# Graph network with two layers: 80 instead of 72 node tiles counted, 80 instead of 108 edge blocks gathered

## The chip, the cores and the metric

One core of one Trainium2 chip runs the whole program. Times are device microseconds of one execution. The kernel before takes 6933.1 us, the median of 3 runs (6923.75 to 6956.05).

## What is computed

The graph has 12500 nodes with 64 features and 400000 edges, sorted by target `dst`, each with 32 features; on the mean 32 edges end in a node. Cut to what matters:

```python
edge_index = jnp.stack([src, dst])
h = relu(layernorm(x))
x = x + L0(h, edge_index, edge_attr_32, ...)   # messages by an MLP with layer norm, summed by target, update
h = relu(layernorm(x))
x = x + L1(h, edge_index, W1, b1, W2, b2)

def L1(x, edge_index, W1, b1, W2, b2):         # the second layer
    src, dst = edge_index
    agg = segment_sum(x[src], dst, num_segments=x.shape[0])
    h = x + agg                                # (1 + 0) * x + agg
    return maximum(h @ W1 + b1, 0) @ W2 + b2
```

The change is about `agg` of the second layer.

## The kernel before

The program is a row of stages with a barrier between them: setup, the first layer's messages, the update of the nodes, the second layer's sums, and its MLP. Each stage is written as one instruction list per engine (PE, ACT, DVE, POOL, SP), and semaphores with counted values hold these together. The order of the work on each engine is written out by hand.

The second layer's sums go into `cT`, the nodes' features with the nodes along the columns. There are two ways to a sum, and both run at once.

**Counted tiles.** The last `TILES` = 72 of the 98 tiles of 128 nodes each (from tile `T0`) get their sums without a gather. For each tile a matrix of counts (source by target) is made: the keys of up to 64 edges a node lie in `keyl` and `keyh`; DVE makes one-hots of them in 8 groups of 8 (`one_hot_pairs`, L1675 and L1677), PE multiplies these in 16 chunks of 4 matmuls (`pairs`, L1619), ACT copies each chunk's counts from PSUM to `cnt` (L1568). PE then multiplies the counts of the tile before with the nodes' features, split into three bf16 parts (`product`, 100 matmuls at L1598, spread over chunks 2 to 15), ACT copies the result (`raw_sums`, L1560, at chunk 0), PE turns it and adds its parts (`turn`, L1609, at chunk 4), and DVE adds it to `cT` (`add_tile`, L1665, after group 5). Pairs write two PSUM buffers in turn, so the pairs of a chunk wait for ACT's copy of the chunk two before; the one-hots have two buffers also.

**Gathered blocks.** The nodes before tile `T0` get their sums from the first `ITER * GN` = 36 * 3 = 108 blocks of 1024 edges. ACT writes a block's indices (`index`, L792), POOL issues 8 indirect DMAs of 128 rows each (L740), DVE makes the one-hots of the targets in a window of 40 nodes (`hots`, L779), PE multiplies them in 4 fp32 products, 8 matmuls in the profile (`window_sums`, L772), and DVE adds even and odd halves to the window of `cT` (`add_block`, L812 and L816). Edges of these blocks that belong to a counted tile are marked so that no column matches.

The loop's body is two tiles, `s` = 0 and 1, with three blocks. Where the blocks' steps stand in it is in four tables: `SUMS` gives PE's chunk of each block's sum (block 0 at chunk 8 of tile 0, blocks 1 and 2 at chunks 3 and 13 of tile 1), `NEXT` ACT's chunk of the index for the next round, `HOTS` and `ADDS` DVE's group of one-hots and adds. A block's buffers are one of three (`gat`, one-hots), its sums one of two PSUM buffers.

In the update stage before, POOL gathers the tiles' keys (`node_edges`, L1253, one indirect DMA a tile, 16 tiles a chunk of the stage, so 8 in the last chunk), in between the copies that feed PE (L1262); DVE masks them (L1419, L1423), PE turns them (L1306), and ACT copies them to `keyl` and `keyh` (L1363).

Of the kernel before, what the change touches and what calls it, by code (L numbers as in the profile page):

```python
# [16 lines left out]
def build_gnn(nc, x, src, dst, src_rows, dst_rows, dst_heads, head_cols, edge_quads, W1, b1, g1, be1, W2, b2, Wu, bu, gn, bn, M1, c1, M2, c2, out):  # L17
# [8 lines left out]
    BLOCKS, BC = src.shape[1], src.shape[2]  # L26
    EB = 128 * BC
    UN = 4
# [6 lines left out]
    T = N // TP  # L35
    Q = 4
    CH = 20 if T % 20 == 0 else Q
    CHUNKS = T // CH
    BQ = CH // Q
# [3 lines left out]
    COLS = dst_rows.shape[1] - 1  # L43
    E = COLS * 128
    SLOTS = 64
    NT = -(-N // 128)
    TILES = 72
    T0 = NT - TILES
    ITER = TILES // 2
    GN = 3  # L50
    HEAD = 8
    HQ = 20
    KC = COLS // 125
# [2 lines left out]
    GPS = 64 // GP  # L56
    GW = 128
    assert EB == 8 * 128 and COLS == 125 * KC and (HEAD * KC) % HQ == 0 and COLS % CHUNKS == 0 and ITER * GN <= BLOCKS
    assert CHUNKS == BQ and GN < UN and NT <= 98 and TILES % 2 == 0 and 4 * T <= 512 and (BLOCKS - 1) * BC < COLS <= BLOCKS * BC
    assert BC % 4 == 0 and T % CH == 0 and CH % Q == 0 and F == 64 and ED == 32 and TP * Q <= 512  # L60

    ctx = ExitStack()
    with ctx:
# [180 lines left out]
        def wait(eng, semaphore, value):  # L244

            if not isinstance(value, int) or value > 0:
                eng.wait_ge(semaphore, value)  # L247
# [567 lines left out]

            return v.tensor_tensor(to, to, of[F:2 * F, WIN:2 * WIN], ALU.add)  # L816

        def before(j):

            return 1 if j == 0 else 2  # L820

        DB = 2 * UN

        def lagged(e, j, lag):
# [663 lines left out]
        k_add = sem("l1_sums_added")  # L1488
# [12 lines left out]

        CHS = 16
        FIRST_PART = 2
        SUMS = ({8: 0}, {3: 1, 13: 2})
        NEXT = ({10: 0}, {5: 1, 15: 2})
        HOTS = ({6: 1}, {4: 2, 7: 3})
        ADDS = ({1: -1, 6: 0}, {3: 1})
        TURN_AT, ADD_AT = 4, 5

        def two(body):  # L1510
# [15 lines left out]
        def first(d, n):  # L1526

            return isinstance(d, int) and d < n

        with nc.Block() as block:  # L1530
# [16 lines left out]
            @block.scalar  # L1547
            def _(a):
                def index(r, j):
                    n = r * GN + j  # L1550

                    wait(a, k_sum, n - GN + 1)
                    indices(a, n, 0, j).then_inc(k_idx, 1)

                def raw_sums(d):

                    wait(a, d_sum, d + 1)

                    wait(a, d_turn, d)
                    a.activation(raw[:, :], wide, ACT.Copy).then_inc(d_raw, 1)  # L1560

                def tile(d, s, e):
                    for ch in range(CHS):
                        wait(a, d_use, d * CHS + ch + 1)
                        if ch == 0:

                            wait(a, d_sum, d - 1)
                        a.activation(cnt[0:TP, s, ch * 8 * T:(ch + 1) * 8 * T].rearrange("p (b k) -> p b k", b=2),  # L1568
                                     built[ch % 2][0:TP, :, :], ACT.Copy).then_inc(d_copy, 1)
                        if ch == 0 and not first(d, 2):  # L1570
                            raw_sums(d - 2)
                        if ch in NEXT[s] and not (isinstance(e, int) and e == ITER - 1):
                            index(e + 1, NEXT[s][ch])
                with a.If(flagged(a) == 0):
                    for j in range(GN):
                        index(0, j)
                    tiles(a, tile)
                    raw_sums(TILES - 2)
                    raw_sums(TILES - 1)

            @block.tensor
            def _(pe):
                def sums(r, j):
                    n = r * GN + j
                    wait(pe, g_gat[j], r * (16 * BC) + L0_ROWS + 16 * BC)
                    wait(pe, k_oh, n + 1)

                    wait(pe, k_add, n + 1 - before(j))
                    window_sums(pe, j, gat[:, j, :, :], agl[j % 2]).then_inc(k_sum, 1)

                def product(d, s, lo, hi):
# [32 lines left out]
                def tile(d, s, e):  # L1624
                    for ch in range(CHS):
                        pairs(d, ch)
                        if ch == TURN_AT and not first(d, 2):
                            turn(d - 2)
                        if ch in SUMS[s]:
                            sums(e, SUMS[s][ch])  # L1630
                        if ch >= FIRST_PART and not first(d, 1):
                            parts = CHS - FIRST_PART
                            product(d - 1, 1 - s, (ch - FIRST_PART) * T // parts, (ch - FIRST_PART + 1) * T // parts)
# [7 lines left out]
            def _(v):  # L1641
                def hots(r, j):
                    n = r * GN + j

                    wait(v, k_sum, n + 1 - GN)
                    one_hot(v, j, block_of(rel_all, n)).then_inc(k_oh, 1)

                def add_block(r, j, groups):
                    n = r * GN + j

                    wait(v, k_sum, n + 1)
                    wait(v, k_add, n)
                    wait(v, d_add, groups)
                    to = window_of(v, n)
                    add_even(v, to, agl[j % 2]).then_inc(k_even, 1)
                    v.wait_ge(k_even, n + 1)
                    add_odd(v, to, agl[j % 2]).then_inc(k_add, 1)

                def add_tile(d, blocks):
                    wait(v, d_turn, d + 1)  # L1660
                    wait(v, k_add, blocks)
                    wait(v, d_add, d)
                    at = (T0 + d) * 128
                    to = cT[0:F, at:at + GW] if isinstance(d, int) else cT[0:F, bass.ds(at, GW)]
                    v.tensor_tensor(to, to, turned, ALU.add).then_inc(d_add, 1)  # L1665
# [14 lines left out]
                def tile(d, s, e):  # L1680
                    for g in range(GPS):
                        one_hot_pairs(d, g)
                        if g in ADDS[s]:
                            j = ADDS[s][g]
                            if j >= 0:

                                add_block(e, j, d - 1 if g > ADD_AT else d - 2)
                            elif not first(e, 1):
                                add_block(e - 1, GN - 1, d - 2)
                        if g == ADD_AT and not first(d, 2):  # L1690
                            add_tile(d - 2, e * GN + (0 if s == 0 else 2))
                        if g in HOTS[s]:
                            j = HOTS[s][g]
                            if j < GN:
                                hots(e, j)
                            elif not (isinstance(e, int) and e == ITER - 1):
                                hots(e + 1, 0)
                with v.If(flagged(v) == 0):
                    hots(0, 0)
                    tiles(v, tile)  # L1700
                    add_block(ITER - 1, GN - 1, TILES - 2)
                    add_tile(TILES - 2, ITER * GN)
                    add_tile(TILES - 1, ITER * GN)

# [131 lines left out]
```

## Time and profile before

| | us |
|---|---|
| Median of 3 runs | 6933.1 |
| The profiled execution | 6930.31 |
| Its span, first to last instruction | 6928.6 |
| Setup, first layer and update, to the first pairs of the second layer | 5067.9 |
| The second layer's sums, 72 tiles | 1678.1 |
| The second layer's MLP | 182.6 |
| PE / PEld / DVE / ACT / POOL busy over the span | 4087.1 / 3298.2 / 2515.7 / 1807.5 / 4280.7 |

A window's row gives its length, then for each engine the busy time and the number of instructions, the clock that was granted to PE as a share of full speed (1.00 is 2.4 GHz, 0.50 is 1.2 GHz), and the DMA traffic. In a timeline a row is an engine's instructions of one line in a row: start, length, engine, line, what was written and read, their number, and in brackets the idle time before them with what ended it. PEld is the weight load that overlaps PE. The tiles of the second layer's sums can be told apart by their pairs, L1619: 64 matmuls a tile, 4 a chunk, with no product between those of chunks 0 and 1.

### The profile page before, as it was taken

What the parts mean: (1) busy time and instruction counts of PE and PEld (TensorE: products, weight loads), DVE (VectorE), ACT (ScalarE), POOL (GpSimd) and SP (SyncE); (2) the same over time, 40 slices, a digit from 0 to 9 for tenths busy, and PEclk for the clock granted to TensorE, in tenths of its full rate; (3) what the DMA queues carried; (4) which work ended last, traced back from release to release, by engine and by line L of the source; (5) the groups of instructions that cost most, each with busy time, mean ns of one, the idle gap of its engine ahead of it and who ended that gap; (6) DMA issues with size and microseconds to landing.
All of it is one profiled execution on the core that took longest, in us unless ns stands there. A gap on an engine that the chain in (4) does not pass through costs nothing. (4 is left out here: it accounts for less than half of the span.)

```text
span 6928.6 us, 75131 instructions
## 1 busy us (share of the span) xinstructions
PE 4087.1 (59%) x24926; PEld 3298.2 (48%) x24926; DVE 2515.7 (36%) x5227; ACT 1807.5 (26%) x2517; POOL 4280.7 (62%) x4190
## 2 busy tenths in 40 slices
PE   5344544544554544555455455456658888788789
PEld 4233333433443433333334333335547777777776
DVE  5222222222222222222222222223656666566551
ACT  1011111111111111111111111111246555555551
POOL 3766666666666666666666666664456655556551
PEclk9556656666665666666566666666579999999995
DMA  2111111111111111111111111111110000000001
GB/s 84 42 34 34 34 34 34 35 33 34 34 35 33 35 34 34 35 34 35 33 34 34 33 35 35 33 34 23 40 23 18 18 17 16 17 17 17 17 17 34
DMA packets 257339, 216.92 MB, mean 31 GB/s; under 512 B 139070, under 2 KB 189563, under 8 KB 256617
## 3 DMA queue, kind: packets, MB, share of 16 engines
q0 software_dynamic: 133248, 136.74, 9.1%
q1 hardware_dynamic: 123881, 77.59, 3.9%
q8 instruction: 106, 1.74, 0.1%
q14 instruction: 104, 0.85, 0.0%
HBM read 199.53 MB, written 14.40 MB: 31 GB/s over the span
## 5 line engine op out<-in xcount | busy, mean ns | idle before, releaser
L740 POOL DMA_INDIRECT gat<-layer_rows,idx x3992 | 4050.5, 1015 | 2172.5 <-issue 1207.8
L765 PE MATMUL ps<-w2d,edge_buffers 128*128 128x128 f32 x3128 | 718.5, 348 | 868.9 <-issue 853.6
L1008 DVE TENSOR_TENSOR edge_buffers<-ps,gat 128x512 f32<-128x512 f32 x391 | 270.5, 692 | 2454.5 <-remote 1428.9
L1568 ACT ACTIVATE node_buffers<-ps 125x800 bf16<-125x800 f32 x1152 | 947.0, 838 | 703.8 <-PE ps L1619 553.5
L765 PEld LDWEIGHTS ps<-w2d,edge_buffers 128*128 128x128 f32 x3128 | 561.7, 241 | 1071.1 <-issue 1070.6
L772 PE MATMUL ps<-one_hots,edge_buffers 128*128 128x80 f32 x3128 | 604.4, 326 | 563.8 <-issue 543.2
L772 PEld LDWEIGHTS ps<-one_hots,edge_buffers 128*128 128x128 f32 x3128 | 593.4, 252 | 645.2 <-issue 615.5
L748 PE MATMUL ps<-w1e,edge_buffers 128*128 128x256 f32 x1564 | 616.0, 509 | 395.8 <-issue 263.1
L967 ACT ACTIVATE edge_buffers<-ps,gcol 128x512 f32<-128x512 f32 x391 | 302.6, 774 | 2088.1 <-remote 1730.9
L1619 PE MATMUL ps<-node_buffers 128*128 128x200 bf16 x4608 | 644.3, 265 | 333.3 <-ACT node_buffers L1568 188.3
L1598 PE MATMUL ps<-edge_buffers,node_buffers 125*128 125x192 bf16 x7200 | 811.5, 256 | 1.7 <-issue 1.2
L1598 PEld LDWEIGHTS ps<-edge_buffers,node_buffers 125*128 125x128 bf16 x7200 | 704.7, 142 | 16.5 <-issue 14.8
L1675 DVE TENSOR_TENSOR node_buffers<-iol,node_buffers 128x1024 bf16<-128x1024 bf16 x576 | 399.3, 693 | 633.4 <-PE ps L1619 454.1
L748 PEld LDWEIGHTS ps<-w1e,edge_buffers 128*128 128x128 f32 x1564 | 366.1, 255 | 521.9 <-issue 484.1
L1619 PEld LDWEIGHTS ps<-node_buffers 128*128 128x128 bf16 x4608 | 412.6, 102 | 420.0 <-issue 256.4
L755 PE MATMUL ps<-ident,node_buffers 128*128 128x128 f32 x1564 | 354.9, 329 | 402.5 <-issue 396.3
L1677 DVE TENSOR_TENSOR node_buffers<-ioh,node_buffers 128x1600 bf16<-128x1600 bf16 x576 | 567.8, 986 | 0.0
L974 ACT ACTIVATE edge_buffers<-ps 128x512 f32<-128x512 f32 x391 | 233.0, 596 | 976.7 <-remote 795.6
L755 PEld LDWEIGHTS ps<-ident,node_buffers 128*128 128x128 f32 x1564 | 241.1, 182 | 446.0 <-issue 443.3
L812 DVE TENSOR_TENSOR cT<-cT,ps 64x40 f32 x499 | 92.9, 186 | 901.8 <-remote 615.8
L953 ACT ACTIVATE node_buffers<-edge_buffers 128x2048 f32<-128x2048 f32 x98 | 187.2, 1910 | 837.1 <-DVE edge_buffers L1008 717.2
L1031 DVE TENSOR_TENSOR node_buffers<-edge_buffers,st 128x512 f32<-128x512 f32 x391 | 267.7, 685 | 3.3
(186 smaller groups left out, 2952.4 us busy)
## 6 DMA issues: line engine op xcount, KB each, us to landing
gat<-layer_rows,idx POOLq DMA_INDIRECT x3992
edge_buffers<-in_edge_quads SPq DMA_DIRECT2D x391, 128.0 KB
node_buffers<-in_x SPq DMA_DIRECT2D x5, 625.0 KB
layer_rows<-node_buffers SPq DMA_DIRECT2D x25, 125.0 KB
residual_rows<-node_buffers SPq DMA_DIRECT2D x5, 625.0 KB
layer_rows<-node_buffers SPq DMA_DIRECT2D x5, 625.0 KB
node_buffers<-residual_rows POOLq DMA_DIRECT2D x25, 125.0 KB, 4.4
out<-node_buffers SPq DMA_DIRECT2D x25, 125.0 KB
```

The source lines that it names most:

```text
L740: pool.indirect_dma_start(out=gat[:, j, c, :], out_offset=None, in_=table[:, :], in_offset=bass.IndirectOffsetOnAxis(ap=idx[:, half, j, c: ...
L748: mm = pe.matmul(o[:, k * 4 * F:(k + 1) * 4 * F], ea[:, j, k, :], w1e[:, :], start=True, stop=True)
L755: mm = pe.transpose(o[:, k * 128:(k + 1) * 128], zn[:, j, 2 * k:2 * k + 2, :].rearrange("p c f -> p (c f)"), ident[:, :])
L765: mm = pe.matmul(o[:, k * 128:(k + 1) * 128], hT[:, j, k * 128:(k + 1) * 128], w2d[:, :], start=False, stop=(k == PAIRS - 1), skip_group_c ...
L772: mm = pe.matmul(to[:, 0:2 * WIN], rows_of[:, 2 * k:2 * k + 2, :].rearrange("p c f -> p (c f)"), oh[:, j, 2 * k:2 * k + 2, :].rearrange("p ...
L967: a.activation(hT[:, s, :], tp[(j - HID) % 2][:, 0:PAIRS * 128], ACT.Silu, bias=gcol[:, 1:2], scale=gcol[:, 0:1]).then_inc(g_h, 1)
L1008: v.tensor_tensor(zb[:, j // UN % 2, s, :, :], zp[j % 2][:, 0:BC * F].rearrange("p (c f) -> p c f", c=BC), gat[:, s, :, :], ALU.add).then_ ...
L1568: a.activation(cnt[0:TP, s, ch * 8 * T:(ch + 1) * 8 * T].rearrange("p (b k) -> p b k", b=2), built[ch % 2][0:TP, :, :], ACT.Copy).then_inc ...
L1598: mm = pe.matmul(wide, cnt[0:TP, s, t:t + (GW - 1) * T + 1:T], hparts[:, t, :, :].rearrange("p k f -> p (k f)"), start=(t == 0), stop=(t = ...
L1619: mm = pe.matmul(built[ch % 2][:, i // 2, (i % 2) * 2 * T:(i % 2 + 1) * 2 * T], ohl[:, ch // 2 % 2, k // 2, :, k % 2], ohk[:, ch // 2 % 2, ...
L1675: v.tensor_tensor(ohl[:, g % 2, :, :, :], iol[:, :, :].unsqueeze(1).broadcast_to([128, GP // 2, 128, 2]), spread(keyl, d, g, 128), ALU.is_ ...
L1677: v.tensor_tensor(ohk[:, g % 2, :, :, :], ioh[:, :, :].unsqueeze(1).broadcast_to([128, GP // 2, 2 * T, 2]), spread(keyh, d, g, 2 * T), ALU ...
```

## The change

80 tiles are counted, from tile 18 on, and 80 blocks gathered, two a loop body: block `s` in tile `s`, through two buffers. In each tile PE takes the sum at chunk 1 instead of 8, 3 or 13, ACT the next round's index at chunk 3, DVE the adds after group 2 and the next one-hots after group 4. The add of a tile's sums waits for the block of the same tile. The separate add of the last block behind the loop is gone. The keys take 8 tiles more.

```diff
-    TILES = 72
+    TILES = 80
     T0 = NT - TILES
     ITER = TILES // 2
-    GN = 3
+    GN = 2
...
-        def before(j):
-
-            return 1 if j == 0 else 2
...
-        SUMS = ({8: 0}, {3: 1, 13: 2})
-        NEXT = ({10: 0}, {5: 1, 15: 2})
-        HOTS = ({6: 1}, {4: 2, 7: 3})
-        ADDS = ({1: -1, 6: 0}, {3: 1})
+        SUM_AT, NEXT_AT, BLOCK_AT, HOT_AT = 1, 3, 2, 4
         TURN_AT, ADD_AT = 4, 5
...
-                        if ch in NEXT[s] and not (isinstance(e, int) and e == ITER - 1):
-                            index(e + 1, NEXT[s][ch])
+                        if ch == NEXT_AT and not (isinstance(e, int) and e == ITER - 1):
+                            index(e + 1, s)
...
-                    wait(pe, k_add, n + 1 - before(j))
+                    wait(pe, k_add, n + 1 - GN)
...
-                        if ch in SUMS[s]:
-                            sums(e, SUMS[s][ch])
+                        if ch == SUM_AT:
+                            sums(e, s)
...
-                def add_block(r, j, groups):
+                def add_block(r, j, d):
                     n = r * GN + j
 
                     wait(v, k_sum, n + 1)
                     wait(v, k_add, n)
-                    wait(v, d_add, groups)
+                    wait(v, d_add, d - 2)
...
-                        if g in ADDS[s]:
-                            j = ADDS[s][g]
-                            if j >= 0:
-
-                                add_block(e, j, d - 1 if g > ADD_AT else d - 2)
-                            elif not first(e, 1):
-                                add_block(e - 1, GN - 1, d - 2)
+                        if g == BLOCK_AT:
+                            add_block(e, s, d)
                         if g == ADD_AT and not first(d, 2):
-                            add_tile(d - 2, e * GN + (0 if s == 0 else 2))
-                        if g in HOTS[s]:
-                            j = HOTS[s][g]
-                            if j < GN:
-                                hots(e, j)
+                            add_tile(d - 2, e * GN + s + 1)
+                        if g == HOT_AT:
+                            if s == 0:
+                                hots(e, 1)
                             elif not (isinstance(e, int) and e == ITER - 1):
                                 hots(e + 1, 0)
                 with v.If(flagged(v) == 0):
                     hots(0, 0)
                     tiles(v, tile)
-                    add_block(ITER - 1, GN - 1, TILES - 2)
                     add_tile(TILES - 2, ITER * GN)
                     add_tile(TILES - 1, ITER * GN)
```

## Rows read from the trace of the kernel before

**Rows 1.** Windows of stages: us, busy (x instructions) per engine, PEclk, DMA

```profile
5067.90:5133.80 65.90, 36.64 (x252) 28.59 (x253) 27.48 (x40) 25.67 (x34) 43.86 (x40) 0.63 0.09 21
5133.80:6715.10 1581.30, 1283.75 (x12558) 1177.93 (x12557) 972.15 (x1485) 923.50 (x1277) 952.22 (x824) 0.92 0.08 17
6715.10:6746.00 30.90, 27.57 (x301) 26.08 (x299) 12.50 (x22) 14.19 (x20) 0.00 (x0) 0.99 0.01 3
6746.00:6928.60 182.60, 178.82 (x500) 114.84 (x500) 19.32 (x50) 33.90 (x50) 33.09 (x25) 0.50 0.19 36
```

**Rows 2.** Windows of single tiles; engines PE, PEld, DVE, ACT, POOL

```profile
5530.58:5550.01 19.43, 16.73 (x181) 15.46 (x180) 14.10 (x23) 13.34 (x20) 11.81 (x11) 1.00 0.07 15
5550.01:5574.35 24.34, 18.09 (x188) 16.27 (x187) 14.04 (x22) 13.17 (x19) 14.52 (x14) 1.00 0.09 20
5574.35:5592.85 18.50, 16.56 (x182) 15.48 (x179) 14.08 (x23) 13.32 (x20) 12.20 (x10) 1.00 0.08 16
6234.07:6250.93 16.86, 16.22 (x180) 15.47 (x179) 14.07 (x23) 13.43 (x20) 12.83 (x10) 1.00 0.08 18
6368.26:6392.71 24.45, 19.76 (x180) 18.34 (x178) 13.59 (x22) 13.00 (x18) 11.25 (x10) 0.83 0.05 12
...
6715.06:6732.13 17.07, 16.58 (x182) 15.84 (x181) 11.98 (x20) 12.84 (x17) 0.00 (x0) 1.00 0.02 4
```

**Rows 3.** Waits, 6715.06 to 6732.13: waiting, released by, us, times, longest

```profile
PE ps L1619 <- ACT node_buffers L1568: 0.5, 1, 0.5
```

**Rows 4.** Waits, 5550.01 to 5574.35

```profile
ACT node_buffers L1568 <- PE ps L1619: 6.7, 6, 2.0
...
PE ps L1619 <- ACT node_buffers L1568: 5.5, 5, 2.0
```

**Rows 5.** Timeline from 5584.4, in the tile from 5574.35

```profile
5584.49 0.53 PE L1619 MATMUL ps<-node_buffers 128*128 128x200 bf16 x4
...
5586.29 0.95 POOL L740 DMA_INDIRECT gat<-layer_rows,idx  x1 [0.30 <-issue]
5586.49 0.84 ACT L1568 ACTIVATE node_buffers<-ps 125x800 bf16<-125x800 f32 x1 [2.50 <-PE ps L1619]
```

**Rows 6.** Timeline of PE in the last tile, without gathers

```profile
6716.51 0.54 PE L1619 MATMUL ps<-node_buffers 128*128 128x200 bf16 x4 [0.49 <-ACT node_buffers L1568]
...
6723.44 0.75 PE L1598 MATMUL ps<-edge_buffers,node_buffers 125*128 125x192 bf16 x7
...
6724.39 0.82 PE L1598 MATMUL ps<-edge_buffers,node_buffers 125*128 125x192 bf16 x8
```

**Rows 7.** Timeline of POOL: a run of 8 gathers, and the next one's start

```profile
5560.84 0.94 POOL L740 DMA_INDIRECT gat<-layer_rows,idx  x1 [3.33 <-ACT idx L792]
...
5570.58 0.94 POOL L740 DMA_INDIRECT gat<-layer_rows,idx  x1 [0.30 <-issue]
5575.63 0.94 POOL L740 DMA_INDIRECT gat<-layer_rows,idx  x1 [4.11 <-ACT idx L792]
```

**Rows 8.** Timeline of DVE and PE: a group of one-hots, a block's sums

```profile
5258.12 0.69 DVE L1675 TENSOR_TENSOR node_buffers<-iol,node_buffers 128x1024 bf16<-128x1024 bf16 x1 [3.51 <-PE ps L1619]
...
5258.73 0.99 DVE L1677 TENSOR_TENSOR node_buffers<-ioh,node_buffers 128x1600 bf16<-128x1600 bf16 x1
...
5259.27 1.04 PE L772 MATMUL ps<-one_hots,gat 128*128 128x80 f32 x8
...
5260.15 1.06 PE L1598 MATMUL ps<-edge_buffers,node_buffers 125*128 125x192 bf16 x6
```

**Rows 9.** Timeline of PE: the first block's sums

```profile
5080.96 1.99 PE L772 MATMUL ps<-one_hots,gat 128*128 128x80 f32 x8 [5.64 <-DMA gat<-layer_rows,idx]
```

**Rows 10.** Timeline of the update stage's last chunks: ACT, and DVE's masks

```profile
4992.42 0.38 ACT L1329 ACTIVATE node_buffers<-ps 125x256 f32<-125x256 f32 x1 [4.50 <-PE ps L1284]
...
5019.81 1.22 DVE L1419 TENSOR_TENSOR node_buffers<-iol,deg 128x1024 bf16<-128x1024 bf16 x1
...
5047.58 0.68 DVE L1419 TENSOR_TENSOR node_buffers<-iol,deg 128x512 bf16<-128x512 bf16 x1
```

More of the change, by code:

```diff
@@ L58, in build_gnn @@
     assert EB == 8 * 128 and COLS == 125 * KC and (HEAD * KC) % HQ == 0 and COLS % CHUNKS == 0 and ITER * GN <= BLOCKS
-    assert CHUNKS == BQ and GN < UN and NT <= 98 and TILES % 2 == 0 and 4 * T <= 512 and (BLOCKS - 1) * BC < COLS <= BLOCKS * BC
+    assert CHUNKS == BQ and GN == 2 and NT <= 98 and TILES % 2 == 0 and 4 * T <= 512 and (BLOCKS - 1) * BC < COLS <= BLOCKS * BC
     assert BC % 4 == 0 and T % CH == 0 and CH % Q == 0 and F == 64 and ED == 32 and TP * Q <= 512
```

## Prediction

> **What bounds the kernel now.** I read the table of stretches first [rows 1]. 1678.1 of the 6928.6 us are the second layer's aggregation, from 5067.9 to 6746.0. Its 72 tiles of 16 chunks run between two barriers, so what a tile takes more or less arrives in full at the end; the MLP behind it (182.6 us, PE busy 178.8) is one chain on PE that the edit does not touch. From the third tile to the last one's start it is 1581.3 us for 69 tiles, 22.9 us each, with 824 gather instructions, 12 a tile. No engine fills it: PE 81%, DVE 61%, ACT 58%, POOL 60%.
>
> So what takes the rest? I took windows of single tiles [rows 2]. Tiles of nearly the same work differ by half. The one from 6234.07 has one block sum, 10 gathers, and nothing late: 16.86 us. The one from 6715.06 is the last: its two sums still come, but no gather is left, and it takes 17.07 us to its last pairs, about 17.8 to where a next tile would begin. The others have 10 to 14 gathers and take 18.5 to 24.5 us. Two things are to be seen: time grows with gathers, and where the granted clock is 0.83 it grows again (24.45 against 18.50 us, both with 10 gathers).
>
> The waits [rows 3, 4] say what is late. In the tile without gathers PE waited 0.5 us for ACT's copies; in the tile from 5550.01 it waited 5.5 us for them, and ACT 6.7 us for PE. Each waits for the other, which is no full engine but a late hand-over. The timeline shows one [rows 5]: the pairs of 5584.49 end at 5585.02, yet ACT's copy of them begins at 5586.49, after 2.50 us of idle, amid a run of gathers. Without gathers [rows 6] the chunks follow each other every 0.95 us (products at 6723.44 and 6724.39). I therefore read the stage as PE's chain of chunks plus a loss that comes with gathers. That is a correlation; why the hand-over is late I can't say.
>
> **The price of a run of gathers.** A clean pair of tiles is 16.86 + 17.8 = 34.7 us. The pair 5530.58 to 5574.35 took 43.77 us at clock 1.00, and its three blocks' gathers come in runs of 8 with 3 to 4 us between them [rows 2, 7]: (43.77 - 34.7) / 3 = 3.0 us a run. The tile from 5574.35 has one late hand-over, at the end of the run that began 1.3 us into it: 18.50 - 16.86 = 1.6 us. Over the whole stretch, slow clock included, a pair takes 45.8, a loss of 11.1 us, 3.7 us a block. So a run costs 1.6 to 3.7 us, and nothing in the tile of 16.86 us.
>
> **Part by part, in a tile.** (a) 80 blocks in place of 108: one sum and one run of 8 gathers a tile instead of one and a half. A sum is 8 matmuls, 0.88 us of PE (5259.27 to 5260.15, [rows 8]). (b) The sum moves to chunk 1. PE idles there already: the pairs of chunk 2 wait for ACT's copy, 0.49 us before 6716.51 [rows 6]. So half of the sum falls into that hole, and a clean tile is 16.86 - 0.5 = 16.4 us. (c) DVE adds the block after its group 2. It starts that group when chunk 1's pairs are done and needs 0.69 + 0.99 us for it [rows 8], by which time the 0.88 us of sums are over: its wait is near 0. Queued behind it on DVE are the later groups, one needed every 1.9 us (two chunks) for 1.68 us of work; the block's two short adds and the one-hots of group 4 take that slack, at worst 0.2 us a tile, in the range. (d) The index at chunk 3 releases POOL at once (the sum it waits for was two chunks before); 8 gathers take some 11 us (5560.84 to 5571.52, [rows 7]) and are wanted nearly two tiles later, so PE waits for rows only at the start. (e) A sum's wait for the add two blocks back and the tile's add's wait for this tile's block are met a tile, or three groups, before: 0. (f) Eight tiles more, whole, with all they cost.
>
> (g) The loss. One run a tile, with some 7 us of rest after it. It will start near chunk 4, later than the run that cost 1.6 and earlier than the one in the middle of a tile, which cost most. I take 2.4, between 1.6 and 3.0. A tile is 16.4 + 2.4 = **18.8 us**.
>
> **Start, end, and the stage before.** The first two tiles took 65.9 us [rows 1]. PE stood 5.64 us there for the first gathered block, at chunk 8 [rows 9]; now it meets that wait at chunk 1, with about 6 us of pairs still undone: 71.9. The end, 30.9 us, loses one sum and one separate add: 29.6. The update stage has 8 more key gathers, all in its last chunk. PE needs 4.88 us for a fifth of that chunk (4.50 + 0.38, [rows 10]) and has 2 gathers beside it on POOL; 3 with the copy would take about 3 x 1.25 + 0.61 = 4.4 on a free POOL, more where DVE is busy: 0 to 2 us. Then mask, turns and key copies cover 16 tiles instead of 8: DVE's 0.68 us become 1.22 [rows 10], its product and ACT's two key copies double likewise, ahead of the last middle part. Together 0 to 5, taken as 3. Two DVE operations over the gathered targets shrink, by less than 0.5 us.
>
> **The sum.** 6928.6 - (65.9 + 1581.3 + 30.9) + (71.9 + 77 x 18.8 + 29.6) + 3 = 6802.6 us of span. The profiled execution took 6930.3, 1.7 more than its span, and the median of three is 2.8 above it: 6802.6 + 1.7 + 2.8 = **6807 us**. Break-even is (1678.1 - 71.9 - 29.6 - 3) / 77 = 20.4 us a tile, a loss of 4.0.
>
> **The rivals.**
> - The loss belongs to the tile, not to its gathers (PE, ACT and DVE passing chunks at this density). Then each tile keeps 11.1 / 2 = 5.6 us: 22.0 a tile, 77 x 3.2 = 246 us more, 7053. Its place is the hand-over of pairs to copies; it decides from a loss of 4.0 us a tile. Against it: the last tile, with everything but gathers, lost nothing. For it: that is one tile, and another took 16.86 us with 10 gathers. 7%. The Trainium skill, SBUF — State Buffer, section Who interferes with whom, takes this side: PE and ACT never wait on anyone, it says, and DMA never contends with a compute engine. By that, fewer gathers would give nothing back.
> - The phase is bad. In the tile from 5550.01 the loss is 24.34 - 17.8 = 6.5 us; about 2 of it came early, with the end of the run before, and 4.5 with the run in the tile's middle. If each run costs 4.5: 20.9 a tile, +162, 6969. Against: the pair's other two runs cost the remaining 4.6. 7%.
> - The clock keeps falling to half, as around the row of 0.83, and the average of 3.7 stays: 20.1 a tile, +100, 6907. Against: it was 1.00 in the three tiles from 5530.58, whose runs are apart, as all will be. For: it was 0.92 over the stretch. 15%.
> - Late hand-overs need two runs close together and mostly vanish: 17.2 a tile, 6684. For: 16.86 us with 10 gathers. 10%.
> - The change doesn't do what it says: if block 80 began before node 18 x 128 = 2304, the general path would run. At 32 edges a node it begins near node 2560. 0%.
>
> **How the numbers follow.** The forecast has 61%: 6807, by itself 6746 (loss 1.6) to 6860 (loss 3.1). The range that leaves out 2 in 10 is 6700 to 6925: it takes in the clock case and the forecast's ends, and leaves out the two slow cases and most of the vanishing one. 0.5% (35 us) is about what a measurement can tell from no change. Faster by more: the forecast, the vanishing case and half of the clock case, 0.78. Within 0.5%: the other half and a part of the phase case, 0.11. Slower: the rest, 0.11.
>
> **What would show it.** PE's pairs: 80 x 64, and 18.8 us from tile to tile. In a steady tile 8 gathers, one sum at chunk 1, the hole of 0.49 us gone. Late hand-overs only while POOL gathers, one or two a tile, near chunks 10 to 12. Granted clock above 0.92. The first two tiles 6 us longer, the MLP unchanged. It is wrong if tiles take 20.4 us or more with 8 gathers each, if DVE's add waits over 0.5 us, or if PE waits for gathered rows in a steady tile.

## The result: slower, and the profile after

The changed kernel takes 7010.06 us, the median of 4 runs (6991.88 to 7012.79), beside 6928.43 (6900.88 to 6956.05) for the kernel before: a ratio of 1.0112, with a 95% interval of 1.0068 to 1.0157. The forecast was 6807. The profiled execution took 6991.88 us, its span is 6990.0.

The windows of the stages, as in [rows 1]: first two tiles, steady tiles, last tile, MLP.

```profile
5076.80:5130.60 53.80, 29.98 (x245) 23.88 (x246) 27.15 (x39) 25.75 (x34) 32.80 (x29) 0.64 0.08 18
5130.57:6778.45 1647.88, 1365.36 (x13709) 1264.21 (x13707) 1052.83 (x1541) 1030.60 (x1386) 652.80 (x611) 0.93 0.05 12
6778.50:6807.00 28.50, 26.30 (x292) 25.02 (x289) 11.74 (x19) 14.27 (x20) 0.00 (x0) 1.00 0.01 2
6807.00:6990.00 183.00, 178.61 (x500) 114.86 (x500) 19.31 (x50) 33.86 (x50) 33.00 (x25) 0.50 0.19 36
```

The span grew by 61.4 us: 8.9 before the second layer, 66.6 in the steady tiles (1647.88 against 1581.3), 0.4 in the MLP, less 12.1 at the start and 2.4 at the end. The steady part is 77 tiles of 21.40 us, where 18.8 was forecast: 77 x 2.6 = 200 us, and the forecast missed by 7010 - 6807 = 203. The other terms nearly cancel: 18.1 us less at the start and 1.1 at the end than forecast, 5.9 more before the second layer, 0.4 in the MLP, and 15.6 because the median execution lies further above the span of the profiled one than before (20.1 us, where 4.5 was taken over). POOL's busy time fell from 952 to 653 us there, and the time did not follow.

Windows of single tiles, as in [rows 2]:

```profile
5520.97:5544.00 23.03, 19.06 (x181) 17.45 (x180) 13.73 (x21) 13.39 (x19) 8.16 (x8) 0.85 0.05 11
...
5563.62:5585.13 21.51, 16.74 (x181) 15.53 (x179) 13.74 (x21) 13.36 (x19) 8.15 (x8) 1.00 0.06 12
5585.13:5602.69 17.56, 16.42 (x180) 15.52 (x179) 13.29 (x21) 13.02 (x19) 9.88 (x8) 1.00 0.06 13
6762.41:6778.45 16.04, 16.04 (x181) 15.56 (x179) 13.61 (x21) 13.40 (x18) 0.00 (x0) 1.00 0.01 2
```

The last row is a tile with its sum and without gathers: 16.04 us, PE busy for all of it. The others hold exactly 8 gathers. Two of them, at clock 1.00 both, differ by 4 us. Look at POOL's column: the same 8 instructions were busy 8.15 us in the slow tile and 9.88 in the fast one. Tile by tile, 39 of the 77 ran at clock 1.00 and took 19.98 us on the mean; the other 38, at 0.875 on the mean, took 22.86. So at full clock the late hand-overs cost 3.9 us a tile, and where the lower clock comes in the loss is 6.8. How much of the difference is the clock, and how much that these tiles have more late hand-overs, isn't separated.

The waits of the tile from 5520.97 (who waits, for whom, us, times, longest) have the form of [rows 4]:

```profile
ACT node_buffers L1561 <- PE ps L1612: 9.5, 10, 2.1
DVE node_buffers L1669 <- PE ps L1612: 9.4, 7, 3.2
...
PE ps L1612 <- issue: 2.9, 2, 1.7
```

And its timeline has the late hand-over of [rows 5]:

```profile
5530.55 0.54 PE L1612 MATMUL ps<-node_buffers 128*128 128x200 bf16 x4
...
5531.58 0.94 POOL L740 DMA_INDIRECT gat<-layer_rows,idx  x1 [0.30 <-issue]
...
5531.88 0.84 ACT L1561 ACTIVATE node_buffers<-ps 125x800 bf16<-125x800 f32 x1 [1.38 <-PE ps L1612]
...
5532.84 0.53 PE L1612 MATMUL ps<-node_buffers 128*128 128x200 bf16 x4 [1.17 <-issue]
```

The pairs end at 5531.09, the copy starts 0.8 us later, and the next pairs 1.17 us late. There are several of these in one run of gathers; the one in [rows 5] stood alone in its tile.

The rest went as planned. The timeline of PE and DVE around chunk 1:

```profile
5521.77 1.04 PE L772 MATMUL ps<-one_hots,gat 128*128 128x80 f32 x8
...
5522.64 0.53 PE L1612 MATMUL ps<-node_buffers 128*128 128x200 bf16 x4
...
5523.75 0.19 DVE L812 TENSOR_TENSOR cT<-cT,ps 64x40 f32 x1
```

Neither the pairs behind the sum nor DVE's add waited.

### The profile page after: what moved, and what is told of

The parts are those of the page before. It is cut to its first block and busy times, and to the rows that moved or that the text cites. A ratio compares the mean times of both kernels' runs of the same rounds, so it can differ in the third digit from the quotient of the medians.

```text
span 6990.0 us, 77493 instructions
## 1 busy us (share of the span) xinstructions
PE 4145.5 (59%) x26094; PEld 3378.7 (48%) x26094; DVE 2595.6 (37%) x5279; ACT 1916.5 (27%) x2627; POOL 3969.9 (57%) x3974
## 5 line engine op out<-in xcount | busy, mean ns | idle before, releaser
L740 POOL DMA_INDIRECT gat<-layer_rows,idx x3768 | 3730.8, 990 | 2535.8 <-issue 1127.8
L1561 ACT ACTIVATE node_buffers<-ps 125x800 bf16<-125x800 f32 x1280 | 1054.3, 838 | 649.8 <-PE ps L1612 541.1
L1591 PE MATMUL ps<-edge_buffers,node_buffers 125*128 125x192 bf16 x8000 | 900.2, 256 | 0.0
L1612 PE MATMUL ps<-node_buffers 128*128 128x200 bf16 x5120 | 711.1, 264 | 312.9 <-issue 168.8
L1591 PEld LDWEIGHTS ps<-edge_buffers,node_buffers 125*128 125x128 bf16 x8000 | 781.3, 142 | 16.4 <-issue 13.5
L1669 DVE TENSOR_TENSOR node_buffers<-iol,node_buffers 128x1024 bf16<-128x1024 bf16 x640 | 443.5, 693 | 606.8 <-PE ps L1612 481.0
L1612 PEld LDWEIGHTS ps<-node_buffers 128*128 128x128 bf16 x5120 | 461.1, 102 | 390.8 <-issue 318.1
L1671 DVE TENSOR_TENSOR node_buffers<-ioh,node_buffers 128x1600 bf16<-128x1600 bf16 x640 | 630.5, 985 | 0.0
```

What stands on the lines that cost most here:

```text
L740: pool.indirect_dma_start(out=gat[:, j, c, :], out_offset=None, in_=table[:, :], in_offset=bass.IndirectOffsetOnAxis(ap=idx[:, half, j, c: ...
L1591: mm = pe.matmul(wide, cnt[0:TP, s, t:t + (GW - 1) * T + 1:T], hparts[:, t, :, :].rearrange("p k f -> p (k f)"), start=(t == 0), stop=(t = ...
L1612: mm = pe.matmul(built[ch % 2][:, i // 2, (i % 2) * 2 * T:(i % 2 + 1) * 2 * T], ohl[:, ch // 2 % 2, k // 2, :, k % 2], ohk[:, ch // 2 % 2, ...
L1669: v.tensor_tensor(ohl[:, g % 2, :, :, :], iol[:, :, :].unsqueeze(1).broadcast_to([128, GP // 2, 128, 2]), spread(keyl, d, g, 128), ALU.is_ ...
L1671: v.tensor_tensor(ohk[:, g % 2, :, :, :], ioh[:, :, :].unsqueeze(1).broadcast_to([128, GP // 2, 2 * T, 2]), spread(keyh, d, g, 2 * T), ALU ...
```

## The experiments

Three readings were to be told apart: the loss belongs to the tile (PE, ACT and DVE at this density); it belongs to what the gathers transfer; or it belongs to POOL's gather instructions and how closely they follow each other. "Loss" is a tile's time less the 16.04 us of a clean one. Most kernels ran once; their times stand beside those of the kernel before on the same chip, which took 6914 to 6971 us. A tile's time is the mean of the 76 or 77 steady ones, if nothing else is said.

**No gathers, half of them.** Edits of POOL's `step`, and of PE's wait for the rows:

```diff
-                    gather(pool, htab, 0, j, g_gat[j])
...
-                    wait(pe, g_gat[j], r * (16 * BC) + L0_ROWS + 16 * BC)
```

> The changed kernel without the second layer's 640 gathers: POOL issues none, PE doesn't wait for rows, and the block sums multiply whatever lies in the buffers, so the second layer's gathered sums are left out. A tile took 21.5 us with gathers, 16.0 us where none was left. Theory 1, the late hand-overs come with the gathers: 16.0 to 16.3 us in every tile, granted clock 1.00, some 77 x 5.4 = 415 us less than the changed kernel, about 6580 us. Theory 2, the loss belongs to the tile: 20 to 22 us a tile, over 6900 us.

Measured: 6549.35 us (before: 6971). Windows of a tile and of 76:

```profile
5421.91:5437.95 16.04, 16.04 (x181) 15.55 (x180) 13.64 (x21) 13.51 (x19) 0.00 (x0) 1.00 0.00 0
...
5117.15:6336.19 1219.04, 1219.04 (x13531) 1182.26 (x13530) 1034.53 (x1521) 1026.35 (x1368) 0.00 (x0) 1.00 0.00 0
```

1219.04 / 76 = 16.04 us, PE busy for every one of them, clock 1.00. The density of the tile costs nothing: that rival is out, though its 7053 us had come within 43 us of the result.

```diff
-                    gather(pool, htab, 0, j, g_gat[j])
+                    for c in range(BC // 2):
+                        pool.indirect_dma_start(
+                            out=gat[:, j, c, :], out_offset=None, in_=htab[:, :],
+                            in_offset=bass.IndirectOffsetOnAxis(ap=idx[:, 0, j, c:c + 1], axis=0)).then_inc(g_gat[j], 16)
...
-                    wait(pe, g_gat[j], r * (16 * BC) + L0_ROWS + 16 * BC)
+                    wait(pe, g_gat[j], r * (8 * BC) + L0_ROWS + 8 * BC)
```

> The changed kernel with 4 of the 8 gathers of each block; the other four columns' rows are left out (old rows are multiplied). Theory 1a, each gather costs the same (5.4 / 8 = 0.7 us): 18.7 us a tile. Theory 1b, a run costs little until several gathers have gone before (the first two or three of a run had nothing late behind them): at most 17.3 us a tile. Theory 2: still 20 us or more.

Measured: 6653.61 us, 17.3 a tile. Four gathers in a row cost 1.3 us, eight 5.4: half the gathers, a quarter of the loss. It is no price per gather.

**Bytes or instructions.** With 16 rows a gather instead of 128:

```diff
-                    gather(pool, htab, 0, j, g_gat[j])
+                    for c in range(BC):
+                        pool.indirect_dma_start(
+                            out=gat[0:16, j, c, :], out_offset=None, in_=htab[:, :],
+                            in_offset=bass.IndirectOffsetOnAxis(ap=idx[0:16, 0, j, c:c + 1], axis=0)).then_inc(g_gat[j], 16)
```

> The changed kernel with 8 gathers a block at the old pace, but of 16 rows each instead of 128 (the other 112 partitions' rows are left out, old ones are multiplied). Theory A, it is the transfers that stand in the way of PE's hand-overs when they come close together: an eighth of the rows, nothing late, 16.0 to 16.3 us a tile. Theory B, it is POOL's issuing of one gather behind another: 20 us or more as with full gathers.

Measured: 7185.68 us (before: 6924), slower than with all rows. Its tiles:

```profile
5639.92:5665.52 25.60, 18.95 (x181) 17.83 (x180) 13.68 (x21) 13.39 (x19) 7.09 (x8) 0.80 0.01 1
5159.21:6971.88 1812.67, 1403.23 (x13532) 1307.99 (x13530) 1041.14 (x1521) 1017.70 (x1368) 566.00 (x600) 0.87 0.01 1
```

1 GB/s is moved instead of 12, and a tile takes 1812.67 / 76 = 23.9 us: a loss of 7.8 in place of 5.4. So it is not the transfer. What did change is the pace: 8 of these come in 9.2 to 10.2 us in most tiles, 8 of the full ones in 10.1 to 11.2.

The full 128 rows' worth of bytes by plain loads, issued by SP, POOL issuing none; and by plain loads that POOL issues:

```diff
-                    gather(pool, htab, 0, j, g_gat[j])
...
-                    wait(pe, g_gat[j], r * (16 * BC) + L0_ROWS + 16 * BC)
+                    wait(pe, k_rows[j], r * (16 * BC) + 16 * BC)
...
+                    wait(sp, k_idx, n + 1)
+                    for c in range(BC):
+                        sp.dma_start(gat[:, j, c, :], htab[c * 128:(c + 1) * 128, :]).then_inc(k_rows[j], 16)
```

> The changed kernel with each gather replaced by a plain load of 128 rows of the same table, of the same bytes into the same buffer, issued by SP in runs of 8; POOL issues nothing (so the gathered rows are left out and wrong ones are summed). Theory A, the bytes written beside PE's work: a loss stays, 17 us a tile or more. Theory B, POOL's issuing, or the descriptors that it writes: 16.0 to 16.3 us.

Measured: 6547.77 us, 16.04 a tile.

```diff
-                    gather(pool, htab, 0, j, g_gat[j])
+                    for c in range(BC):
+                        pool.dma_start(gat[:, j, c, :], htab[c * 128:(c + 1) * 128, :]).then_inc(g_gat[j], 16)
```

> The changed kernel with its gathers replaced by plain loads of 128 rows of the table, of the same bytes, issued by POOL in runs of 8 (the gathered rows are left out). From SP the same loads cost nothing (16.04 us). Theory B1, POOL making descriptors for any DMA: 20 us or more a tile. Theory B2, only indirect ones, whose indices POOL reads: 16.0 to 16.5 us.

Measured: 6576.74 us. The window of 76 tiles, and then, from the groups by line between 5200 and 6300, POOL's (count, busy us, mean ns, idle time before and what ended it):

```profile
5143.87:6362.96 1219.09, 1219.09 (x13532) 1182.28 (x13530) 1034.51 (x1521) 1026.01 (x1368) 316.33 (x600) 1.00 0.06 16
```

```profile
L1533 POOL DMA_DIRECT2D gat<-layer_rows x547 | 288.4, 535 | 803.9 <-ACT idx L792 790.8 <-issue 13.1
```

Eight plain DMAs in a run of 4.2 us, twice as close as the gathers, lose nothing. The loss needs POOL's indirect form. (These loads read consecutive rows; the same bytes at scattered addresses without an indirect instruction weren't tried.)

**Spread out.** Each gather waits for one more pair of ACT's copies, so that one comes every two chunks, some 1.9 us:

```diff
-                    gather(pool, htab, 0, j, g_gat[j])
+                    for c in range(BC):
+                        if not (isinstance(r, int) and r == 0):
+                            wait(pool, d_copy, (2 * r - 2 + j) * CHS + 4 + 2 * c)
+                            wait_alone(pool, "gpsimd")
+                        pool.indirect_dma_start(
+                            out=gat[:, j, c, :], out_offset=None, in_=htab[:, :],
+                            in_offset=bass.IndirectOffsetOnAxis(ap=idx[:, 0, j, c:c + 1], axis=0)).then_inc(g_gat[j], 16)
```

> The changed kernel with all 8 gathers of a block, but each held back until ACT has copied two more chunks, so that they are spread over a tile and never stand in a run. Theory 1a, a loss for each gather: 21 us a tile as before. Theory 1b, the loss comes from gathers close to one another: under 18 us a tile, some 250 us less than the changed kernel.

Measured: 6572.44 us. 16.04 a tile, but every 14th takes 17.3. It was then timed:

> The spread gathers again, timed in rounds against the kernel before: 16.04 us a tile, 6570 us, a ratio near 0.948 and outside any doubt.

Measured: 6599.56 us (6590.66 to 6611.6) against 6954.17: ratio 0.9488, 95% interval 0.9451 to 0.9526. It leaves nothing out, and gathers what the changed kernel gathers. Its window of 76 tiles:

```profile
5154.91:6382.10 1227.19, 1221.96 (x13530) 1182.79 (x13529) 1038.28 (x1521) 1023.12 (x1368) 570.53 (x603) 1.00 0.07 16
```

And the waits of 5200 to 6300, first of the changed kernel, then of this one:

```profile
ACT node_buffers L1561 <- PE ps L1612: 361.7, 381, 2.1
...
PE ps L1612 <- issue: 108.4, 85, 3.1
PE ps L1612 <- ACT node_buffers L1561: 80.7, 83, 1.9
```

```profile
ACT node_buffers L1567 <- PE ps L1618: 142.5, 340, 1.4
...
PE ps L1618 <- ACT node_buffers L1567: 5.2, 10, 0.7
```

189 us of PE's waits for the hand-over became 5, with all 8 gathers a tile in place. The clock came back with them, from 0.93 to 1.00.

Besides the pace, this edit fixes another thing: each gather starts right behind a copy of ACT. The traces tell the two apart in part. Take each hand-over where ACT already stood idle when a chunk's pairs ended, and call it late if the copy began over 0.3 us after that. Without gathers none of 964 is late. In this kernel 528 fell in the 1.25 us behind a gather's start, spread over all of them. 523 of them were beside a gather that had started over 1.85 us after the one before it, and none was late; the other 5 were beside closer ones, and all 5 were late. In the changed kernel it is 0 of 84 and 38 of 122.

Those 5 are the longer tiles. Five times in the stage POOL stands still for 4.1 us (why, no run shows) and then catches up. This is the first time; the pairs end at 5312.01:

```profile
5309.66 1.16 POOL L1536 DMA_INDIRECT gat<-layer_rows,idx  x1 [4.14 <-ACT node_buffers L1567]
...
5311.13 0.94 POOL L1536 DMA_INDIRECT gat<-layer_rows,idx  x1 [0.30 <-ACT node_buffers L1567]
...
5312.38 1.24 POOL L1536 DMA_INDIRECT gat<-layer_rows,idx  x1 [0.31 <-issue]
...
5313.28 0.84 ACT L1567 ACTIVATE node_buffers<-ps 125x800 bf16<-125x800 f32 x1 [1.34 <-PE ps L1618]
```

Closer together: in pairs every four chunks, and one every one and a half chunks on the mean (the releases lie one and two chunks apart in turn).

```diff
-                            wait(pool, d_copy, (2 * r - 2 + j) * CHS + 4 + 2 * c)
+                            wait(pool, d_copy, (2 * r - 2 + j) * CHS + 4 + 4 * (c // 2))
```

> The changed kernel with all its gathers, two back to back after every fourth copy of ACT. The mean rate is that of the spread gathers (nothing lost, 16.04 us), the runs are 2 long. Runs of 4 cost 1.4 us. If what counts is how many gathers stand directly behind one another, and two don't suffice: 16.0 to 16.2 us. If every back-to-back gather costs the same (1.4 / 3 = 0.47): four of them a tile, 17.9 us.

Measured: 6601.94 us, 16.46 a tile, a loss of 0.4 with two gathers in 2.4 to 2.8 us, four times a tile. Here 23 of 411 hand-overs beside the wider spaced gathers were late too, so the distance to the gather just before isn't all that counts.

```diff
-                            wait(pool, d_copy, (2 * r - 2 + j) * CHS + 4 + 2 * c)
+                            wait(pool, d_copy, (2 * r - 2 + j) * CHS + 4 + 3 * c // 2)
```

> The changed kernel with each of a block's gathers held back by 1.5 chunks, so at least 1.43 us apart at clean speed (1.25 us is POOL's own pace, 1.9 us cost nothing). If only POOL's full pace does harm: 16.0 to 16.3 us a tile. If the loss falls off with distance: between, 17 to 19 us. In the 72-tile kernel at 1.3 us apart 4.4 us a tile stayed.

Measured: 6612.05 us; 16.04 in most tiles, every 14th 19.0, 16.3 on the mean. POOL's groups from 5200 to 6300, of this kernel and then of the changed one:

```profile
L1536 POOL DMA_INDIRECT gat<-layer_rows,idx x540 | 762.9, 1413 | 338.1 <-ACT node_buffers L1567 247.5 <-issue 90.6
```

```profile
L740 POOL DMA_INDIRECT gat<-layer_rows,idx x411 | 439.7, 1070 | 672.4 <-ACT idx L792 555.3 <-issue 117.1
```

POOL is busy 69% of the time here and 40% in the changed kernel, which loses 5.4 us a tile. Busy POOL is not what costs. Nor did the gathers come 1.43 us apart, as intended: they were stretched, three in four stood 0.30 us behind the one before, and half of them started 1.9 us or more after it. So this kernel tests nothing between 1.4 and 1.9 us; it shows that gathers without a rest between them cost next to nothing when they are long.

**16 rows, spread.**

```diff
-                    gather(pool, htab, 0, j, g_gat[j])
...
+                            wait(pool, d_copy, (2 * r - 2 + j) * CHS + 4 + 2 * c)
...
+                            out=gat[0:16, j, c, :], out_offset=None, in_=htab[:, :],
+                            in_offset=bass.IndirectOffsetOnAxis(ap=idx[0:16, 0, j, c:c + 1], axis=0)).then_inc(g_gat[j], 16)
```

> The 16-row gathers (23.9 us a tile in runs of 8; 112 partitions' rows are left out) spread one to two chunks. If pace is what matters: 16.0 to 16.1 us a tile. If a 16-row gather is dear by itself: more than 17 us.

Measured: 6574.67 us, 16.05 in most tiles, 17.1 or more in every 15th, 16.14 on the mean. The instructions that cost 7.8 us a tile in a row cost 0.1 apart. Number and kind are equal; only when each one starts differs.

**Another place for the run.** The index, and with it the run, at another chunk:

```diff
-        SUM_AT, NEXT_AT, BLOCK_AT, HOT_AT = 1, 3, 2, 4
+        SUM_AT, NEXT_AT, BLOCK_AT, HOT_AT = 1, 11, 2, 4
```

> The changed kernel with the next round's index at chunk 11 instead of 3, so that the run of gathers starts near chunk 12 and ends near chunk 6 of the next tile, over the tile's border. In the kernel before the runs that began at chunk 12 cost 2.2 us, the run in the middle of a tile 4.5, and in the changed kernel those at chunk 4 cost 5.4 and 1.9 to 3.6. Theory 3, the place of the run in the tile sets its price: 18.2 to 19 us a tile, about 6790 us. Theory 1a: 21.5 as before, about 7000 us.

Measured: 6738.20 us, 18.25 a tile, runs of 10.4 to 12.0 us, the median 11.8.

With `NEXT_AT` = 14:

> The changed kernel with the index at chunk 14: the runs start near chunk 15 and lie over the first half of a tile, as the runs of the kernel before that cost 1.6 us. If the place decides: 17.6 to 18 us a tile. If only the number in a row counts: 21.5.

Measured: 6860.99 us, 19.8 a tile, runs of 10.8 to 11.7 us, the median 11.2.

With `NEXT_AT` = 7:

> The changed kernel with the index at chunk 7, so runs of 8 gathers start near chunk 8. Index at 3 gave 21.5 us a tile, at 11 18.2. If the place decides: between, or as dear as the run in the middle of a tile in the kernel before (4.5, 20.5 us a tile). If only the number in a row counts: 21.5.

Measured: 6581.95 us (before: 6935), 16.4 a tile. Timed:

> The index at chunk 7, timed in rounds against the kernel before: 6580 to 6610 us, a ratio of 0.945 to 0.955, the same as with spread gathers within a few tenths of a per cent (16.35 against 16.1 us a tile is 20 us).

Measured: 6597.37 us (6588.92 to 6605.35) against 6914.1: ratio 0.9535, interval 0.9494 to 0.9577. One number gives back what the edit lost and more. The gathers follow each other without a rest here too, yet look at their lengths. POOL's timeline of one run with `NEXT_AT` = 7, then of the run in the changed kernel's slow tile:

```profile
5411.18 1.03 POOL L740 DMA_INDIRECT gat<-layer_rows,idx  x1 [4.03 <-ACT idx L792]
5412.52 1.51 POOL L740 DMA_INDIRECT gat<-layer_rows,idx  x1 [0.30 <-issue]
5414.34 1.47 POOL L740 DMA_INDIRECT gat<-layer_rows,idx  x1 [0.30 <-issue]
...
5422.51 0.94 POOL L740 DMA_INDIRECT gat<-layer_rows,idx  x1 [0.30 <-issue]
```

```profile
5568.72 0.94 POOL L740 DMA_INDIRECT gat<-layer_rows,idx  x1 [8.79 <-ACT idx L792]
...
5574.20 0.94 POOL L740 DMA_INDIRECT gat<-layer_rows,idx  x1 [0.30 <-issue]
5575.45 0.94 POOL L740 DMA_INDIRECT gat<-layer_rows,idx  x1 [0.30 <-issue]
...
5577.95 1.06 POOL L740 DMA_INDIRECT gat<-layer_rows,idx  x1 [0.30 <-issue]
```

12.3 us for eight (5411.18 to 5423.45) against 10.3 (5568.72 to 5579.01). A gather takes 0.94 us by itself, and in these two kernels each that took over 1.01 us, up to 1.77, had DVE at work beside it. (Not each gather beside DVE is stretched: nearly all of the spread ones stay at 0.94 to 0.95.) In the first run they start 1.62 us apart on the mean, in the second 1.32, and over the stage a tile loses 0.3 us there and 5.4 here. Within the changed kernel it is the same: the run of the 17.56 us tile, from 5590.05 to 5602.07, took 12.0.

**The sum's place, with the gathers spread.**

```diff
-        SUM_AT, NEXT_AT, BLOCK_AT, HOT_AT = 1, 3, 2, 4
+        SUM_AT, NEXT_AT, BLOCK_AT, HOT_AT = 8, 10, 5, 4
...
+                            wait(pool, d_copy, (2 * r - 2 + j) * CHS + 11 + 2 * c)
```

> The spread gathers with the sum at chunk 8 and the index at chunk 10 (the places of block 0 in the kernel before), the adds after group 5. It measures the moved sum alone, with no loss from gathers on top: if the hole before chunk 2 takes half of the sum, as forecast, 16.5 to 16.9 us a tile against 16.04, some 35 to 70 us more in all; if the place is indifferent, 16.04.

Measured: 6653.32 us, 17.0 a tile, 0.9 more than with the sum at chunk 1. That isn't the sum's place alone, since the index and DVE's adds moved with it. From 5200 to 6300 two waits are new, about one of each a tile:

```profile
PEld ps L1618 <- DVE node_buffers L1677: 60.1, 87, 0.9
DVE cT L812 <- PE ps L772: 58.0, 60, 1.0
```

DVE stands in its add until the sum comes, and PE then waits for DVE's one-hots. How much of the 0.9 the sum at chunk 1 saves by filling a hole of PE isn't separated.

**The kernel before, with the same edits.**

```diff
-                    gather(pool, htab, 0, j, g_gat[j])
+                    for c in range(BC):
+                        if not (isinstance(r, int) and r == 0):
+                            wait(pool, d_copy, (2 * r - 2) * CHS + 11 + 4 * (j * BC + c) // 3)
+                            wait_alone(pool, "gpsimd")
+                        pool.indirect_dma_start(
+                            out=gat[:, j, c, :], out_offset=None, in_=htab[:, :],
+                            in_offset=bass.IndirectOffsetOnAxis(ap=idx[:, 0, j, c:c + 1], axis=0)).then_inc(g_gat[j], 16)
```

> The kernel before (72 tiles, 108 blocks) with its gathers spread: one after every 4/3 chunks, 12 a tile, some 1.3 us apart at clean speed, near the 1.25 us at which POOL can issue them. If the distance between gathers sets the loss: little is won, 20 to 22 us a tile, 6800 to 6900 us. If spreading removes it as in the changed kernel: 17.3 us a tile, 6530 us, and then gathering more and counting less would be the better choice.

Measured: 6817.28 us, 43.1 a pair of tiles. 12 gathers in a tile of 17.3 us can be 1.4 us apart at best, which leaves the stretched ones no room. In its trace 3 in 10 started under 1.3 us after the one before. It keeps a loss of 4.3 us a tile; one run of 6817 beside one of 6924 is a small gain.

Then without gathers (the first edit, in the kernel before):

> The kernel before without the second layer's 864 gathers (its gathered sums are left out). A pair of its tiles was put at 34.7 us without a loss and took 45.8. If all of that loss comes with gathers: 34.4 to 34.8 us a pair, about 400 us less than the kernel before.

Measured: 6512.59 us. Windows of a pair of tiles and of 69:

```profile
5451.66:5468.53 16.87, 16.22 (x180) 15.50 (x179) 13.93 (x23) 13.58 (x20) 0.00 (x0) 1.00 0.00 0
5468.53:5486.20 17.67, 17.11 (x189) 16.39 (x187) 13.97 (x22) 13.48 (x19) 0.00 (x0) 1.00 0.00 0
5106.26:6297.17 1190.91, 1149.27 (x12556) 1099.53 (x12555) 962.30 (x1485) 933.70 (x1277) 0.00 (x0) 1.00 0.00 0
```

A clean tile of the kernel before is 1190.91 / 69 = 17.26 us, so its loss was 1581.3 - 1190.9 = 390.4 us with 824 gathers, 0.47 us each. The changed kernel's is 1647.88 - 77 x 16.04 = 412.8 us with 611: 0.68 each. That is where the expected gain went: 213 gathers fewer, each nearly half as dear again. The new place lets them go faster: 1.07 us busy for each gather on the mean, 1.16 before.

## Why the prediction was wrong, step by step

- **The reading of the bound** (PE's chain of chunks plus a loss that comes with gathers) held. It was called a correlation; the kernel without gathers shows the cause. The clean pair of 34.7 us was measured at 34.5.
- **(a), (b)** A clean tile was put at 16.4 us and is 16.04. Right, a little too careful: against the clean tile with one sum in the kernel before (16.87 us) the new places save 0.8 and not 0.5. Which of them saves it isn't separated.
- **(c)** DVE's add does not wait. **(e)** No wait of a sum or an add shows. Both right.
- **(d)** POOL is released at once and no steady tile waits for rows: right. That the place of the index is free was the mistake that step (g) inherits.
- **(f)** Eight more tiles: 80 x 16.04 is 1283 us against 72 x 17.26 = 1243, so more tiles pay only through the loss that fewer gathers avoid.
- **(g) The step that failed.** The loss was put at 2.4 us a tile, the bounds at 1.6 and 3.7; it is 21.40 - 16.04 = 5.4, past the break-even of 4.0. Of the 412.8 us, PE stood 1647.9 - 1365.4 = 282.5, and in the other 130 it was busy longer: 105 of these lie in the 38 tiles at a lower clock, 26 in the 39 at 1.00. Two things were mis-sized, then. At full clock a run cost 3.9 us and not 2.4; and the clock, left at 1.00 in the sum since the runs would be apart, fell in half of the tiles, whose loss is 6.8. I took a run to have a price by its place in the tile and interpolated between three places. The value 4.5, which stood in the text as "the phase is bad", I outvoted by the mean of its pair. The step used the runs' places and never their lengths, which POOL's timeline shows. The run that cost 4.5 is that of [rows 7], 10.7 us long. The one that cost 1.6 goes on behind the last line of [rows 7] thus (kernel before, POOL's timeline):

```profile
5576.88 1.54 POOL L740 DMA_INDIRECT gat<-layer_rows,idx  x1 [0.30 <-issue]
...
5586.29 0.95 POOL L740 DMA_INDIRECT gat<-layer_rows,idx  x1 [0.30 <-issue]
```

From 5575.63 to 5587.24 it is 11.6 us. The slower run was the cheaper one. And the tile of 16.86 us in [rows 2], where 10 gathers cost nothing, has the slowest of the three, though they begin at the same place, 1.3 us into the tile:

```profile
6235.35 0.94 POOL L740 DMA_INDIRECT gat<-layer_rows,idx  x1 [7.13 <-ACT idx L792]
...
6249.94 1.37 POOL L740 DMA_INDIRECT gat<-layer_rows,idx  x1 [0.30 <-issue]
```

  From start to start these ten are 1.62 us apart on the mean; the run that cost 1.6 has 1.52, the one that cost 4.5 has 1.39. The same place had two prices in the kernel before, and the pace told them apart. The experiments put the loss in the same order by the mean distance within runs: 1.26 us cost 7.8 (16 rows), 1.37 cost 5.4 (the changed kernel), 1.47 cost 3.8 and 1.49 cost 2.2 (index at chunks 14 and 11), 1.62 cost 0.3 (chunk 7). The order alone proves nothing, since a late hand-over leaves DVE idle, and idle DVE lets gathers go faster. The spread kernels show the direction: there each gather's start was set by hand, number and kind stayed, and the loss went.
- **The start** was to take 71.9 us and took 53.8. The wait for the first block came at chunk 1 as said, and was longer:

```profile
5087.61 1.99 PE L772 MATMUL ps<-one_hots,gat 128*128 128x80 f32 x8 [9.29 <-DMA gat<-layer_rows,idx]
```

  But the second tile took 15.45 us instead of the half clock and late hand-overs that I had carried over from before. **The end**: 28.5, forecast 29.6. **The MLP**: 183.0, unchanged.
- **The stage before** was to cost 0 to 5 us; the second layer starts 8.9 later. In its last chunk POOL's copies, each behind three key gathers, are the part that can be seen:

```profile
4990.86 0.61 POOL L1258 COPY node_buffers<-cT 128x500 f32<-128x500 f32 x1
...
4996.70 1.16 POOL L1258 COPY node_buffers<-cT 128x500 f32<-128x500 f32 x1
```

  5.84 us from one to the next, where I had 4.4 on a free POOL: one of the three gathers between them took 2.04 us. How much of the 8.9 is this, and how much the stages before, which differ from one execution to the next, wasn't separated.
- **The rivals.** "The loss belongs to the tile" (7%, 22.0 us a tile) came near in numbers and is refuted. The Trainium skill, SBUF — State Buffer, section Who interferes with whom, says that PE and ACT never wait on anyone. It says so of ports of SBUF; the prediction stretched it to the hand-over between the engines. There the runs show otherwise: with POOL's gathers close together PE's work is handed to ACT up to 2 us late, 5.4 us a tile in all, and without gathers never. Whether that is a port or the way a signal takes, no run here shows. "The phase is bad" (7%, 20.9 us a tile, 6969 us) came nearest: its size was right, and the new place was a bad one, though by the pace it allows. "The clock keeps falling" was a part of it, at most some 110 of 413 us (38 tiles, each 2.9 us dearer), as a consequence: the windows without gathers, with plain DMAs and with spread gathers all stand at 1.00.
- **The range** (6700 to 6925) was too narrow because the slow case got 7% when one row of three already spoke for it, and its trigger was not understood; the clock case, at 15%, came true together with it, where the list had each by itself.

**What stays open.** How a gather delays the hand-over, inside the chip; that late hand-overs feed themselves (DVE idle, gathers faster), which is argued from the rows and not tested alone; why POOL stands still for 4.1 us every 14th tile of the spread kernel; whether distances between 1.5 and 1.9 us, set by hand, would do; and whether 108 blocks with their runs at a slow place would be as fast as the spread kernel.

## What to carry to other kernels

Price a background instruction by its pace as well as its number: list its runs with their lengths and what the chain lost in each before moving one, and take one dear run as a warning that a new place may make it the rule. Where a DMA-issuing engine has slack, release its indirect gathers one by one against the consumer's progress; with the change that made a kernel 5% faster than the one before, and moving the index to where another engine slows the gathers did as much. To see whether a cost is the transfer or the instruction, shrink the transfer and swap the instruction's kind: two runs settle it.

## What was not expected of the hardware

- Indirect DMAs issued by POOL in a row, 1.25 us apart at the closest and 1.37 on the mean, go with late hand-overs from PE to ACT, in which the gathered rows have no part: 5.4 us in a tile of 16.04 for 8 of them, 7.8 when they are of 16 rows and 1.15 us apart at the closest, 0.1 when each is held back to some 1.9 us after the last. Plain DMAs from POOL, 0.53 us each and as far apart, do nothing of the kind.
- The length of an indirect DMA hardly depends on its rows: 0.84 us for 16, 0.94 for 128. In runs without a rest it grows where DVE works beside it, to 1.75 us in the changed kernel and up to 2.4 in others.
- A slower POOL made a faster kernel: mean 1070 ns a gather in the changed kernel, 1413 in the one with a release every one and a half chunks, with 7010 and 6612 us in all (the second one run).
